# Adjacency times single operands: fp32 as it stands, on column halves of the array, instead of an fp32r high and low part

## What is computed

```python
u_comm = Wt @ XB - jnp.sum(Wt, axis=1, keepdims=True) * XB       # layer 0, one product with adj
T_curr = L_tilde @ x                                             # layer 1, three products with adj
T_next = 2.0 * (L_tilde @ T_curr) - T_prev
h_neigh = (adj @ X + X) / deg                                    # layer 2, one product with adj
w = mask * jnp.where(pos > 0, DECAY ** (k - pos), 0.0)           # layer 3, ranks of the nonzeros of a row
out = w @ support + bias
```

## Time and profile before

| | |
|---|---|
| runs, us | 3055.67, 3058.36, 3058.33 |
| median, us | 3058.33 |
| span of the profiled execution, us | 3056.1 |
| TensorE busy | 2920.8 us, 96% |
| VectorE busy | 2815.9 us, 92% |
| ScalarE busy | 2355.9 us, 77% |
| read from HBM | 1143.75 MB, 375 GB/s over the span |

### The profile page before, as it was taken

The page is one execution under the profiler, slowest core; times in us unless marked ns, Lnnn a source line. Parts: engine busy times, 40 slices in busy tenths (PEclk is TensorE's granted clock), DMA queues, the critical chain, the costliest instruction groups (busy, mean ns, idle before and its releaser), DMA issues.

```text
span 3056.1 us, 35248 instructions
## 1 busy us (share of the span) xinstructions
PE 2920.8 (96%) x13425; PEld 2157.9 (71%) x13488; DVE 2815.9 (92%) x2385; ACT 2355.9 (77%) x1631; POOL 13.2 (0%) x31
## 2 busy tenths in 40 slices
PE   7999999999999998999989999988989999999998
PEld 5678788887788886888867888766766555555554
DVE  7998999889998889988899988999999899999997
ACT  5887887777776778776787777877877788888887
POOL 0000000000000000000000000000000000000000
PEclk9999999999999999999999999999999999999999
DMA  9999999999999999999999999999999999999996
GB/s 347 392 391 356 398 369 381 374 384 360 377 399 376 372 382 387 400 382 377 378 374 368 383 378 376 381 339 356 397 403 410 352 383 388 384 381 388 377 384 244
DMA packets 158935, 1148.18 MB, mean 376 GB/s; under 512 B 18016, under 2 KB 18256, under 8 KB 19504
## 3 DMA queue, kind: packets, MB, share of 16 engines
q1 hardware_dynamic: 157312, 1143.02, 95.5%
q0 software_dynamic: 1088, 2.48, 0.2%
q10 hardware_dynamic: 368, 0.43, 0.0%
HBM read 1143.75 MB, written 2.10 MB: 375 GB/s over the span
## 4 chain that ended last, share of the span: by engine, by line
PE 68%; DVE 23%; DMA 4%; ACT 3%; issue 2%; SPq 0%; ACTq 0%; DVEq 0%
PE ACC L944 26%; DVE lo L670 18%; PE ACC L951 15%; PE ACC L1073 14%; DMA raw<-in_at 4%; PE PSF L1087 4%; PE PST L1087 4%; ACT hi L476 2%; DVE SV L780 1%; PE PST L967 1%; PE PSF L1053 1%; PE PSF L1028 1%; DVE SV L787 1%; PE PSF L1031 0%; PE PSF L1026 0%
## 5 line engine op out<-in xcount | busy, mean ns | idle before, releaser
L670 DVE TENSOR_TENSOR lo<-raw,hi 128x2048 fp32r<-128x2048 f32 x832 | 1877.2, 2287 | 143.9 <-ACT hi L476 139.0
L476 ACT CAST hi<-raw 128x2048 fp32r<-128x2048 f32 x832 | 1583.5, 1912 | 512.7 <-PE ACC L944 306.2
L944 PE MATMUL ACC<-hi,T 128*128 128x512 f32 x4992 | 1279.3, 393 | 6.2 <-DVE T L628 4.3
L944 PEld LDWEIGHTS ACC<-hi,T 128*128 128x128 f32 x4992 | 934.9, 189 | 207.5 <-DVE T L628 4.6
L951 PE MATMUL ACC<-lo,T 128*128 128x512 f32 x3200 | 884.7, 398 | 92.6 <-DVE lo L670 87.2
L951 PEld LDWEIGHTS ACC<-lo,T 128*128 128x128 f32 x3200 | 590.9, 189 | 280.5 <-DVE lo L670 165.0
L685 DVE SCALAR_TENSOR_TENSOR M<-raw,M 128x512 bf16<-128x512 f32 x1008 | 637.7, 688 | 43.5 <-PE ACC L1073 26.9
L482 ACT ACTIVATE Wf<-ACC,w_bias 128x1024 fp32r<-128x1024 f32 x512 | 568.9, 1115 | 131.0 <-PE ACC L1073 130.4
L1073 PE MATMUL ACC<-M,rank_b 128*128 128x512 bf16 x1969 | 520.5, 383 | 12.2 <-ACT Wf L482 4.6
L1073 PEld LDWEIGHTS ACC<-M,rank_b 128*128 128x128 bf16 x2032 | 159.3, 98 | 268.1 <-issue 136.2
L1087 PE MATMUL PST<-Wf,S 128*128 128x512 f32 x512 | 209.9, 491 | 0.0
(11 more groups left out here) (165 smaller groups left out, 985.3 us busy)
## 6 DMA issues: line engine op xcount, KB each, us to landing
raw<-in_at SPq DMA_DIRECT2D x1088, 1024.0 KB, 6.8
SV<-in_x_cols SPq DMA_DIRECT2D x8, 256.0 KB, 12.1
out<-O POOLq DMA_DIRECT2D x7, 256.0 KB, 6.5
out<-O ACTq DMA_DIRECT2D x1, 256.0 KB, 2.0
w_sb<-in_w POOLq DMA_DIRECT2D x3, 64.0 KB, 9.0
bias<-in_bias_rows ACTq DMA_DIRECT2D x1, 128.0 KB, 9.5
l1w_sb<-in_l_w POOLq DMA_DIRECT2D x2, 64.0 KB, 8.0
rank_f<-in_rank_mats POOLq DMA_DIRECT2D x1, 128.0 KB, 9.7
```

Source lines behind the costliest of these rows:

```text
L476: nc.scalar.copy(hi[:, c % NH], raw[:, c % NR]).then_inc(hi_done, 1)
L670: tt(lo[:, c % NR], raw[:, c % NR], hi[:, c % NH].bitcast(f32), ALU.subtract).then_inc(lo_done, 1)
L944: ins = mm(acc[:, part], w, hi[:, p.c % NH, s, part], start=p.opens and s == 0 and i == 0, stop=False)
```

## The change

Pairs of one operand are no longer split. TensorE reads `raw` as it landed and multiplies in fp32 with 64 columns of weights, the operand as one fp32 number. The even chunk of the pair (s = 0) goes to partitions 0 to 63 of the accumulator, in two matmuls of 512 columns, then the odd chunk (s = 1) to partitions 64 to 127. The two halves are added in the combination as before. Two-operand pairs are left as they are, but for the numbering of the `hi` buffers. A view `XF` of the same bytes as `T` holds the whole operand; the step `st` moves from ScalarE to VectorE and adds high and low part; `operand_parts` writes the whole operand first and lets TensorE go, and the low part is told of by a semaphore of its own, `t_low`.

```diff
+    XF, _ = place("XF", [P, G, 2, 2, D], f32, T_at)
-    ST1, GS_at = place("ST1", [P, Q, 2, D], f32r)
-    ST = [place("ST0", [P, Q, 2, D], f32r, UT_at)[0], ST1]
+    ST1, GS_at = place("ST1", [P, Q, 2, D], f32)
+    ST = [place("ST0", [P, Q, 2, D], f32, UT_at)[0], ST1]
...
+    def two_operands(p):
+        return p.kind == "P" and p.k < 5
+
+    split_no = {}
+    for p in pairs:
+        if two_operands(p):
+            split_no[p.c] = len(split_no)
...
         if k > 1 and kind == "D":
-            due("ACT", c - NP + (2 if r == 0 else 0), "st", k, r)
+            due("DVE", c - NP, "st", k, r)
...
-            nc.gpsimd.memset(T[:, :, 0, 1, D - 1].bitcast(f32), 0.0).then_inc(pool_chain, 1)
+            nc.gpsimd.memset(XF[:, :, 0, 1, D - 1], 1.0).then_inc(pool_chain, 1)
...
             def split_hi(c):
+                n = split_no[c]
                 act.wait_ge(raw_in[c % NR], 16 * (c // NR + 1))
-                if c >= NH:
-                    act.wait_ge(hi_used, c - NH + 1)
-                    act.wait_ge(lo_done, c - NH + 1)
-                nc.scalar.copy(hi[:, c % NH], raw[:, c % NR]).then_inc(hi_done, 1)
+                if n >= NH:
+                    act.wait_ge(hi_used, n - NH + 1)
+                    act.wait_ge(lo_done, n - NH + 1)
+                nc.scalar.copy(hi[:, n % NH], raw[:, c % NR]).then_inc(hi_done, 1)
...
-                    if c:
+                    if c in split_no:
                         split_hi(c)
...
-                link(tt(T[:, g, 1, 0, most], PSF[:, :, most], T[:, g, 0, 0, most].bitcast(f32), ALU.subtract))
-                copy(T[:, g, 0, 1, most], T[:, g, 1, 0, most].bitcast(f32)).then_inc(t_init, 1)
+                copy(XF[:, g, 0, 1, most], PSF[:, :, most]).then_inc(t_init, 1)
+                tt(T[:, g, 1, 0, most], PSF[:, :, most], T[:, g, 0, 0, most].bitcast(f32), ALU.subtract).then_inc(
+                    t_low, 1)
...
             def split_lo(c):
-                p = pairs[c]
-                dve.wait_ge(hi_done, c + 1)
-                tt(lo[:, c % NR], raw[:, c % NR], hi[:, c % NH].bitcast(f32), ALU.subtract).then_inc(lo_done, 1)
+                n = split_no[c]
+                dve.wait_ge(hi_done, n + 1)
+                tt(lo[:, c % NR], raw[:, c % NR], hi[:, n % NH].bitcast(f32), ALU.subtract).then_inc(lo_done, 1)
...
+                elif what == "st":
+
+                    dve.wait_ge(v_done, v_count[k - 1, I])
+                    own = T[:, g, :, u_slot(k)].bitcast(f32)
+                    if k == 3:
+                        dve.wait_ge(pair_done, d_end[d_turn[k, r] - 2] + 1)
+                        dst = ST[d_turn[k, r] % 2][:, :, 0]
+                    else:
+                        dve.wait_ge(pair_done, last_use[k - 1, I] + 1)
+                        dst = XF[:, g, 0, 1 - u_slot(k)]
+                    tt(dst, own[:, :, 0], own[:, :, 1], ALU.add).then_inc(st_done, 1)
...
+            def multiply_one(p):
+                k = p.k
+                acc = ACC[acc_of[k, p.kind, p.r]]
+                pe.wait_ge(raw_in[p.c % NR], 16 * (p.c // NR + 1))
+                for s in range(2):
+                    w = ST[d_turn[k, p.r] % 2][:, 2 * p.pr + s, 0] if k == 3 else XF[:, p.J * Q + 2 * p.pr + s, 0, v_of(k)]
+                    for h in range(2):
+                        part = slice(h * HALF, (h + 1) * HALF)
+                        ins = mm(acc[ph(s), part], w, raw[:, p.c % NR, s, part], start=p.opens, stop=p.closes)
+                ins.then_inc(pair_done, 1)
...
-    pick[D - 1, D] = 1
+    pick[D - 1, D] = pick[P - 1, D] = 1
```

More of the change, by code:

```diff
@@ L156, in graph_layers @@
     c_x, c_bias = [sem(f"c_x{b}") for b in range(NB)], sem("c_bias")
-    intra_done = sem("intra_done")
+    intra_done, t_low = sem("intra_done"), sem("t_low")
     c_hid, c_rest, c_w, c_late = sem("c_hid"), sem("c_rest"), sem("c_w"), sem("c_late")
@@ L366, in graph_layers @@
     dve_sv = numbered("DVE", "diag", "sum")
-    act_st = numbered("ACT", "st")
+    dve_st = numbered("DVE", "st")
     squares = numbered("ACT", "z_sq", "relu", "square", "out_sq")
@@ L504, in step @@
                     nc.scalar.copy(SV[part, cols(I)], ACC[acc_of[k, "D", r]][part, :]).then_inc(sv_act, 1)
[L505 to L514, removed]
                 elif what == "ut":
@@ L585, in step @@
                     out_root(slice(0, r * Q))
-            split_hi(0)
             high_part(0)
@@ L879, in _ @@
                 cx_ready, 1)
-            split_lo(0)
             operand_parts(0)
@@ L918, in operand_there @@
                         pe.wait_ge(v_done, v_count[1, p.J])
+                        pe.wait_ge(t_low, p.J + 1)
                 elif p.kind == "D" or p.k == 5:
-                    pe.wait_ge(st_done, act_st["st", p.k, block_of(p.k, p.J, NB)])
+                    pe.wait_ge(st_done, dve_st["st", p.k, block_of(p.k, p.J, NB)])
                 else:
@@ L924, in multiply @@
             def multiply(p):
[L925 to L934, removed]
                 if p.first_of_block:
@@ L937, in multiply, with multiply_two @@
                 if p.opens:
-                    open_acc(key)
-                pe.wait_ge(hi_done, p.c + 1)
+                    open_acc((p.k, p.kind, p.r))
+                if two_operands(p):
+                    multiply_two(p)
+                else:
+                    multiply_one(p)
+            def multiply_one(p):
[8 more added lines that the diff above has]
+                ins.then_inc(pair_done, 1)
+            def multiply_two(p):
+                acc, n = ACC[acc_of[p.k, p.kind, p.r]], split_no[p.c]
+                g = p.J * Q + 2 * p.pr
+                ws = [[T[:, g + s, t].rearrange("p t d -> p (t d)") for t in range(2)] for s in range(2)]
+                pe.wait_ge(hi_done, n + 1)
                 for s in range(2):
@@ L943, in multiply @@
                             part = slice(h * HALF, (h + 1) * HALF)
-                            ins = mm(acc[:, part], w, hi[:, p.c % NH, s, part],
+                            ins = mm(acc[:, part], w, hi[:, n % NH, s, part],
                                      start=p.opens and s == 0 and i == 0, stop=False)
                 ins.then_inc(hi_used, 1)
-                pe.wait_ge(lo_done, p.c + 1)
+                pe.wait_ge(lo_done, n + 1)
                 for s in range(2):
```

## The result

The changed kernel takes 2970.84 us (median of 4 runs, 2969.36 to 2971.72) against 3058.35 us for the kernel before: a ratio of 0.9714 with a 95% interval of 0.9700 to 0.9728. It is 87 us faster, where 180 us slower was forecast. The span of the profiled execution is 2969.3 us.

The account below looks back on a forecast made before the run. TensorE was taken as the bound outside sweep 5 and the start, VectorE in sweep 5, the DMA close behind. Terms +55 + 83 + 34 + 10 = +182 us on 3056.1 us gave 3238 us; range 3150 to 3610.

Parts of the forecast that it names:

- the number of slots that lie beside each other: One-operand pairs on TensorE: eight fp32 instructions of 0.44 us, overlapping at two places, take 6 instruction times, 2.64 us.
- +55 in sweep 5: Sweep 5, all one-operand pairs: TensorE becomes the bound, 455 us with steps against 400 us before.
- +83 in sweep 1: Sweep 1: 118 us more TensorE work, partly absorbed by idle time and drains, leaves 83 us more.
- +34 in sweeps 2 to 4: Sweeps 2 to 4: 79 us more TensorE work, 15 us a sweep absorbed by gaps, leaves 34 us more.
- +10 for changes between tiles: TensorE switching between whole-array and half-array matmuls: 0.1 to 0.2 us a change, perhaps 80 changes, between 0 and 30 us.
- full overlap: Case where both column halves always run together on TensorE: 4 instruction times, 1.76 us a one-operand pair; chance 0.15.
- The price of a slot: One fp32 instruction of 512 columns on TensorE: 0.44 us, between 0.427 and 0.454, two instructions per matmul call.
- The serial rival: One-operand pairs on TensorE: the halves never overlap, 3.52 us a pair, 3576 us in all; chance 0.35.
- The rival that came: Both column halves run beside each other, VectorE's wait is pure gain up to the DMA: about 2988 us; chance 0.15.
- Its term for sweep 5: Sweep 5 with halves fully side by side: DMA bound at 2.60 us a pair, falls to 375 us (-25).
- The -30 us for sweep 1: Sweep 1 with halves fully side by side: about 30 us shorter, one-operand pairs at 2.60 us.
- -15 for sweeps 2 to 4: Sweeps 2 to 4 with halves fully side by side: 5 us shorter each.

Follow-up runs that it names:

- half_by_pair: Changed kernel with each one-operand pair sent whole to one column half, even pairs to partitions 0 to 63, odd ones to 64 to 127; 3048.84 us.
- one_half: Changed kernel with both chunks of each one-operand pair on partitions 0 to 63, the other half written once per group; 3512.48 us.
- dve_full: Changed kernel plus one unused 128 x 2048 subtraction a pair on VectorE in sweep 5; 3029.24 us (0.9907).
- after: The changed kernel itself, unedited, as profiled after the change; 2970.84 us against 3058.35 us for the kernel before.

## Why the prediction was wrong

**The step that failed is the number of slots that lie beside each other.** I let a matmul start beside the one before it only if that one was on the other half, in the order of the program: 6 slots, 2.64 us a pair. Measured is 4 slots, 1.717 us, whatever the order within a pair. In the changed kernel the odd chunk starts beside the even one, past three of its records that have yet to start; in `half_by_pair` it is again three, with a semaphore wait between, and never more. The error is 384 x 0.92 = 355 us of TensorE work, where my sum had added 315; everything else in it hung on this, +55 in sweep 5 became -45, +83 in sweep 1 became -19, +34 in sweeps 2 to 4 became -20. The +10 for changes between tiles cannot be read apart from these. I had reasoned from starts in order in a trace in which no two neighbours were on different halves. That trace could not show the order of such starts, and I gave the case that came, full overlap, 0.15. The range left it out.

The Trainium skill, "TensorE: Matmul & The Clock Gate", Part 3, says both that column tiles run concurrently and that matmuls start and end strictly in program order. The runs agree with the first (starts 0.005 to 0.059 us apart). The second does not hold here across halves: in `half_by_pair` a transpose starts ahead of three matmuls of the other half, and in `one_half` L953 starts ahead of three L956. Within one half no row here shows it broken.

**The price of a slot** was near: 0.44 forecast, 0.429 measured. fp32 as two instructions with two passes each, read off the transpose, holds. The serial rival was priced at 3576 us and measured at 3512.5; 34 of the 64 us are 384 x 8 x 0.011 for the slot, and the rest is in my allowance for gaps and turns.

**The rival that came** was priced at 2988 us, 17 us too slow. Its term for sweep 5 is mis-sized: I took 403 GB/s from a window of 100 us with a DMA share of 1.00 as the limit. The limit is 421 GB/s, and a reading costs 2.49 us and not 2.60: 144 x 0.11 = 16 us. The trace before showed it already: windows of 20 us in that stretch moved 413, 374, 415 and 417 GB/s, and the mean took in the slow one. The -30 us for sweep 1 came as -19, and -15 for sweeps 2 to 4 as -20.

**What was right**: that VectorE bound sweep 5 (`dve_full` brings its time back and more, if at a lower clock), that the DMA stands close behind, that `st` costs nothing on VectorE (in sweeps 1 to 5 TensorE never waits for it), that two-operand pairs stay at 2.72 us (from 1302.69 to 1305.41 in the changed kernel's timeline) and that stage 6 stays nearly as it is (728.3 us). A turn from the whole array to a half costs little. In the same timeline, of sweep 3, the four L972 before L953 take 1.00 us to the next start at 1163.61 against 0.91 between two-operand pairs, 0.09 us, where I had allowed 0.1 to 0.2.

```profile
1302.69 1.98 PE L965 MATMUL ACC<-hi,T 128*128 128x512 f32 x8
...
1304.51 1.07 PE L972 MATMUL ACC<-lo,T 128*128 128x512 f32 x4
...
1305.41 1.98 PE L965 MATMUL ACC<-hi,T 128*128 128x512 f32 x8
...
1162.61 1.07 PE L972 MATMUL ACC<-lo,T 128*128 128x512 f32 x4
1163.61 2.85 PE L953 MATMUL ACC<-raw,ST 128*64 128x512 f32 x12
```

## What to carry to other kernels

Where a matmul needs only 64 columns of weights, fp32 on both column halves costs no more of TensorE than a split into fp32r parts with 128 columns (1.717 against 1.82 us here), and it takes the splitting off the other engines; the order of the calls may stay simple as long as no more than three matmuls of one half stand unstarted before the first of the other. An engine can bound a stage by its total even if nobody waits for the work that fills it, so look at what stands behind that work in its queue. Where a forecast hangs on a thing that the trace cannot show, both ends of it belong in the range.

## What the runs showed of the hardware

- The two column halves of the array take their matmuls independently: 0.429 us a record of 512 fp32 columns on one half, and two such side by side. A matmul starts past at most three of the other half that stand ahead of it and have yet to start, a semaphore wait between or not (`after`, `one_half`, `half_by_pair`).
- Transposes of 128 fp32 columns on one half run four at a time between the starts of matmuls on the other (`half_by_pair`).
- Weight loads of 64 columns come in twos as well, 0.43 us apart.
- The readings of 1 MB reach 421 GB/s with ScalarE busy 42 of 50 us, and 419 GB/s with VectorE busy 247 of 355 us.
